# Macaron block, Mamba phase: the gated result stays in its PSUM banks, and the output projection moves to the middle of the slot

## What is computed

```python
proj = hidden_states @ W_in.T                      # z, x, B, C, dt
xBC = silu(conv1d(xBC, conv_w, kernel 4) + conv_b)
dt = softplus(dt + dt_bias); A = -exp(A_log)
Y_diag = einsum('bclhn,bcshn,bhcls,bcshp->bclhp', C_c, B_c, Lmat, x_dt)
Y_off  = einsum('bclhn,bhcpn,bhcl->bclhp', C_c, prev_states, exp(A_cum))
y = Y_diag + Y_off + D_param * x                   # x: the skip
g = y * silu(z)                                    # the gate
gn = g * rsqrt(mean(g * g) + eps) * norm_w
return gn @ W_out.T
```

## Time and profile before

| | |
|---|---|
| median of 3 runs | 2416.67 us (2415.77 to 2417.97) |
| the profiled execution: its own time | 2403.61 us |
| its span, first to last instruction | 2401.9 us |
| mean granted TensorE clock | 0.966 |
| the Mamba phase in it | about 380 to 2040 us |
| one group (two slots) in the loop | 47.8 us |

### The profile page before, as it was taken

How to read it: one execution, slowest core, us unless ns; L and a number is a source line. 1 busy time by engine, 2 the same in 40 slices (tenths; PEclk the granted TensorE clock), 3 DMA queues, 4 the chain that set the end, 5 groups by cost and what they waited for, 6 DMA issues and landing times. The chain is left out here.

```text
span 2401.9 us, 43273 instructions
## 1 busy us (share of the span) xinstructions
PE 2168.2 (90%) x11718; PEld 1748.5 (73%) x11718; DVE 1732.9 (72%) x2954; ACT 1430.8 (60%) x2899; POOL 1503.9 (63%) x1242
## 2 busy tenths in 40 slices
PE   5799987899999999999888999999999998579997
PEld 3687765677777777777666777777777776367776
DVE  6432276688888888888877888888888886743226
ACT  5133324777767776777566777677767774513332
POOL 2885341667767776777426777677767774288633
PEclk8999997999999999999999999999999999789999
DMA  9665351443334333333213334333433330266546
GB/s 340 238 188 168 116 157 41 115 113 92 92 103 107 92 97 102 102 92 100 60 39 111 94 90 104 105 95 89 105 105 95 88 105 18 75 241 189 160 135 193
DMA packets 204904, 285.32 MB, mean 119 GB/s; under 512 B 16288, under 2 KB 148458, under 8 KB 204816
## 3 DMA queue, kind: packets, MB, share of 16 engines
q1 hardware_dynamic: 185936, 219.18, 31.8%
q0 software_dynamic: 18880, 65.02, 8.7%
HBM read 225.43 MB, written 58.72 MB: 118 GB/s over the span
## 5 line engine op out<-in xcount | busy, mean ns | idle before, releaser
L2026 PE MATMUL mamba_p_proj<-mamba_xt_lo,mamba_in_hi 128*128 128x512 f32 x1056 | 462.6, 438 | 70.1 <-DVE mamba_xs L1706 52.2
L2028 PE MATMUL mamba_p_proj<-mamba_xt_hi,mamba_in_lo 128*128 128x512 f32 x1056 | 418.4, 396 | 0.0
L2027 PE MATMUL mamba_p_proj<-mamba_xt_hi,mamba_in_hi 128*128 128x512 f32 x1056 | 417.5, 395 | 0.0
L1315 POOL TENSOR_TENSOR mamba_mix<-mamba_mix,mamba_scores 128x512 f32<-128x512 f32 x256 | 372.3, 1455 | 70.0 <-ACT mamba_mix L1507 70.0
L1503 ACT ACTIVATE mamba_mix<-mamba_cum_l,mamba_cum_g 128x128 f32<-128x128 f32 x1024 | 324.5, 390 | 3.9 <-PE mamba_p_diag L2134 2.9
L1701 DVE SCALAR_TENSOR_TENSOR mamba_xs<-mamba_p_proj,mamba_taps,mamba_xs 128x511 f32<-128x511 f32 (+2 forms) x384 | 285.5, 744 | 46.2 <-ACT mamba_xs L1437 26.7
L2026 PEld LDWEIGHTS mamba_p_proj<-mamba_xt_lo,mamba_in_hi 128*128 128x128 f32 x1056 | 202.1, 191 | 129.4 <-DVE mamba_xs L1706 65.0
L1309 POOL TENSOR_TENSOR mamba_xend<-mamba_xdt,mamba_to_end_g 128x512 f32<-128x512 f32 x128 | 135.0, 1055 | 252.2 <-DVE mamba_xdt L1761 252.2
L1732 DVE TENSOR_TENSOR mamba_total<-mamba_p_out,mamba_total 128x512 f32<-128x512 f32 x256 | 176.4, 689 | 151.1 <-PE mamba_p_out L2062 150.9
L1322 POOL TENSOR_TENSOR mamba_decayed<-mamba_state,mamba_exp_last_g 128x256 f32<-128x256 f32 x192 | 181.8, 947 | 157.9 <-DVE mamba_state L1793 155.6
L660 DVE TENSOR_TENSOR ffn_h<-ffn_p_gu,ffn_sil 128x256 f32<-128x256 f32 x110 | 46.8, 426 | 294.3 <-ACT ffn_sil L545 293.9
(11 more groups left out here) (336 smaller groups left out, 5318.1 us busy)
## 6 DMA issues: line engine op xcount, KB each, us to landing
mamba_cum_l<-mamba_cum_rows SPq DMA_DIRECT2D x128, 512.0 KB, 5.6
mamba_rise<-mamba_exp_rows SPq DMA_DIRECT2D x256, 128.0 KB, 3.3
ffn_xs<-slots_in SPq DMA_DIRECT2D x78, 256.0 KB, 2.7
slots_out<-ffn_y SPq DMA_DIRECT2D x78, 256.0 KB, 2.5
mamba_raw_x<-in_t SPq DMA_DIRECT2D x34, 512.0 KB, 7.0
mamba_raw_z<-in_t SPq DMA_DIRECT2D x32, 512.0 KB, 7.8
mamba_raw_out<-out_t SPq DMA_DIRECT2D x32, 512.0 KB, 6.5
slots_out<-ffn_xs SPq DMA_DIRECT2D x1, 9984.0 KB, 42.3
```

The costliest lines, as they stand in the source:

```text
L1315: pool.tensor_tensor(mix[:, c, :, :], mix[:, c, :, :], scores[:, b * CPB + c, :].unsqueeze(1).broadcast_to([P, GH, P]), ALU.mult).then_inc ...
L2026: pe.matmul(bank, in_hi[:, piece, kk, :], xt_lo[:, kk, c], start=(kk == 0), stop=False)
L2027: pe.matmul(bank, in_hi[:, piece, kk, :], xt_hi[:, kk, c], start=False, stop=False)
L2028: last = pe.matmul(bank, in_lo[:, piece, kk, :], xt_hi[:, kk, c], start=False, stop=(kk == KT - 1))
```

## The change

A unit's result stays in the two banks that `diag` wrote, now named p_y: `add_skip`, `add_carry` and `gate` read and write p_y in place, ACT's square and g_hi and DVE's g_lo read it. All of this is done in the unit's own slot. So `diag` of the next unit waits for `gate_low` (s_glo) and no more for `add_skip` (s_y). ACT squares before it rounds. `project_out(U-1)` moves from the end of the slot to after `start(2)`, both `project_z` to after `off(3)`; the queues of the other engines are put in a matching order. A one-element Exp at the end of ACT's slot loads the table of exponentials there.

```diff
 # ACT
             def tap_x(k, gi, b, ct, young=False):
-                    act.wait_ge(s_g, U * CT - 2 * CT + ct + 1)
+                    act.wait_ge(s_y, U * CT - 2 * CT + ct + 1)
...
-            def high(U, gi, b, ct, second=False):
+            def square_and_high(U, gi, b, ct, first=False):
+
+                if ct == 0 and not first:
+                    act.wait_ge(s_pout, U * TPB)
                 act.wait_ge(s_g, U * CT + ct + 1)
-                if not second:
-                    act.wait_ge(s_pout, U * TPB)
-                act.activation(g_hi[:, ct, :], zs[:, b, ct, :], ACT.Copy,
+                act.activation(zs[:, b, ct, :], p_y[:, ct, :], ACT.Square).then_inc(s_sq, 1)
+                act.activation(g_hi[:, ct, :], p_y[:, ct, :], ACT.Copy,
                                scale=norm_w[:, bass.ds(gi * CT + ct, 1)]).then_inc(s_ghi, 1)
 # DVE
-                    dve.tensor_tensor(zs[:, b, ct, :], xs[:, b, ct, :], zs[:, b, ct, :], ALU.mult).then_inc(s_g, 1)
+                    dve.tensor_tensor(p_y[:, ct, :], p_y[:, ct, :], zs[:, b, ct, :], ALU.mult).then_inc(s_g, 1)
...
-                    dve.scalar_tensor_tensor(g_lo[:, ct, :], zs[:, b, ct, :], norm_w[:, bass.ds(gi * CT + ct, 1)],
+                    dve.scalar_tensor_tensor(g_lo[:, ct, :], p_y[:, ct, :], norm_w[:, bass.ds(gi * CT + ct, 1)],
...
-                    dve.scalar_tensor_tensor(xs[:, b, ct, :], xs[:, b, ct, :], skip[:, bass.ds(gi * CT + ct, 1)],
-                                             p_diag[:, ct, :], ALU.mult, ALU.add).then_inc(s_y, 1)
+                    dve.scalar_tensor_tensor(p_y[:, ct, :], xs[:, b, ct, :], skip[:, bass.ds(gi * CT + ct, 1)],
+                                             p_y[:, ct, :], ALU.mult, ALU.add).then_inc(s_y, 1)
...
-                    dve.tensor_tensor(xs[:, b, ct, lo:BLK], xs[:, b, ct, lo:BLK], carry[:, ct, lo:BLK],
+                    dve.tensor_tensor(p_y[:, ct, lo:BLK], p_y[:, ct, lo:BLK], carry[:, ct, lo:BLK],
 # PE
                     if j == 0 and not first:
-                        pe.wait_ge(s_y, U * CT)
+                        pe.wait_ge(s_glo, U * CT)
...
-                else:
-                    project_z(k, gn, bn, 0)
                 if first:
                     diag(1)
+                elif not last:
+                    project_out(k, gp, bp, range(TPB), second)
                 off(3)
                 start(3)
...
+                    project_z(k, gn, bn, 0)
+                    rows(k, gn, bn, 0)
                     project_z(k, gn, bn, 1)
-                    rows(k, gn, bn, 0)
-                    if not first:
-                        project_out(k, gp, bp, range(TPB), second)
-                if not last:
                     rows(k, gn, bn, 1)
```

More of the change, by code:

```diff
@@ L1363, in slot @@
                     decay_scores(U, b, 3)
-                clear(0)
-                next_z(0)
-                next_z(1)
                 this_out(0)
                 this_out(1)
+                clear(0)
+                if not first:
+                    for ct in range(CT):
+                        add_squares(U - 1, 1 - b, ct, second and ct == 0)
                 clear(1)
@@ L1585, in slot @@
                     silu_z(U + 1, 1 - b, 0, first)
-                    if b == 0 and not last_group:
-                        round_x(k, gi, V, 1)
+                for ct in range(CT):
+                    square_and_high(U, gi, b, ct, k == 0 and first)
+                if more:
+                    dt_copy(k + 1, 1)
+                if b == 0 and not last_group:
+                    round_z(k, gi, U, 0)
+                if not last:
                     silu_z(U + 1, 1 - b, 1, first)
-                    exponents(k, gn, bn, 3)
                 if b == 0 and not last_group:
-                    for ct in range(CT):
-                        round_z(k, gi, U, ct)
+                    round_z(k, gi, U, 1)
+                if not last:
+                    act.activation(spare, one[:, :], ACT.Exp)
             def vectors():
@@ L1835, in slot @@
                 next_state(0)
-                if not first:
-                    gate(k, gp, bp)
-                elif k > 0:
-                    finish(k - 1, range(6, T))
                 if b == 1 and not last:
                     stage_cum(k, gn)
+                if first and k > 0:
+                    finish(k - 1, range(6, T))
                 next_rows(0, 1)
@@ L1846, in slot @@
                 next_state(1)
-                if not first:
-                    gate_low(U - 1, gp, 1 - b)
                 next_rows(2, 3)
@@ L1861, in slot @@
                     add_out(1)
-                add_skip(1)
+                if not last:
+                    for t in range(CPB):
+                        add_out(t)
+                next_stats(1)
                 carry_of(3)
@@ L1866, in slot @@
                     add_carry(ct)
-                if not last:
+                gate(k, gi, b)
+                next_rows(6, 7)
+                if last:
+                    for t in range(2, CPB):
+                        add_out(t)
+                        if more:
+                            lns.low(dve, k + 1, T - CPB + t)
+                else:
                     if b == 1:
@@ L1870, in slot @@
                     times_dt(k, gn, bn, 0)
-                if more:
-                    gate(k, gi, b)
-                next_rows(6, 7)
-                for t in range(2 if last else 0, CPB):
-                    add_out(t)
-                    if more:
-                        lns.low(dve, k + 1, T - CPB + t)
-                if more:
-                    gate_low(U, gi, b)
+                gate_low(U, gi)
                 if not last:
```

73 lines of the change are left out of this document (27 added, 46 removed).

## The result

The changed kernel takes 2475.49 us (median of 4 runs, 2468.46 to 2478.83), the kernel before, on the same chip, 2416.57 us (4 runs, 2415.77 to 2417.97): a ratio of 1.024, 95% interval 1.0227 to 1.0253, so 2.4% slower. The profiled execution takes 2474.68 us with a span of 2472.8 and a granted clock of 0.952. Against the profiled execution of before (2403.61) it is 71 us longer, where the medians are 59 apart. The traces tell where the 71 lie. The Mamba phase, from PE's first to its last instruction in it, takes 1683.6 us before and 1737.6 after, 54.0 more. The other 17 us are in the feed-forward layers, whose code is the same (718.2 and 735.3 us in all).

The account below looks back on a forecast made before the run. PE, 90% busy, was taken to set the time. New accumulation waits of +131.7 us, less 68.8 and 4, give +59 us: 2416.7 + 59 = 2476 us, 2.4% slower; own range 2445 to 2504, wider range 2425 to 2504.

Parts of the forecast that it names:

- the named wait: Tile 2 of project_out on PE waits for DVE's accumulation of tile 0: 4.39 us new per slot pair, +131.7 us.
- the wait with b = 0: PE's new accumulation wait in b = 0 slots, halo steps held by POOL: 3.07 us; 1.49 with clean steps.
- What goes: PE's two waits for DVE's convolution before project_z vanish, -68.8 us; half the gate_low waits in batches' last slots, -4 us.
- The wait with b = 1: PE's new wait in b = 1 slots for DVE's accumulation before tile 2 of project_out: 1.32 us.
- its rounding comes after the next x projection; I cost this at nothing: SP's raw_x load still issued at the previous slot's carry, landing in 7.0 us, rounded later: no cost.
- the term of -4: Last slot of a batch: gate_low's late waits for project_out sum to 7.8 us; half taken as gone, -4 us.
- The 13 us carried over: The earlier runs' median stood 13 us above the profiled execution; kept, making 2463 into 2416.7 + 59 = 2476 us.
- The range: The forecast's own 2445 to 2504 us, for 0.7 us less or 0.9 us more waiting per slot pair.
- Gets cheaper but doesn't count.: gate on DVE falls from 1131 ns to 0.7 us with one input in PSUM; worth nothing by itself.
- The end of the slot: diag(0) waits for gate_low's read of p_y: 6.9 us chain hidden behind 9.0 us of PE projections, about 2 spare.
- rival 3: gate_low late for diag(0) on top of the forecast: at 1 us a slot +60, 2536 us; chance 0.06.
- Rival 2: Accumulation isn't waited for, faster: 2344 us; sign turns at a mean new wait of 1.21 us per slot; chance 0.12.

Follow-up runs that it names:

- runs 9 to 11: Changed kernel with DVE's accumulator additions earlier still and each batch's first round_x(0) behind tap_x(1), the middle one with SBUF tiles: 2330.10, 2330.39 and 2330.35 us.
- Run 4: Changed kernel with the small halo steps of ct 1 reading their PSUM bank in place of the SBUF halo tile: 2419.81 us, ratio 1.0015.
- Run 1: Changed kernel with DVE's accumulation of tiles 0 and 1 between the convolution steps of ct 1, except in a batch's last slot: 2366.93 us, ratio 0.9794.
- run 3: Changed kernel with two accumulator additions between the convolution steps of ct 1 in slots with b = 0 alone: 2403.84 us, ratio 0.9954.
- run 2: Changed kernel with two accumulator additions between the convolution steps of ct 1 in slots with b = 1 alone: 2412.96 us, ratio 0.9985.
- run 8: Changed kernel with round_x(0) moved back behind tap_x(1) on ACT in each batch's first slot: 2452.89 us, ratio 1.0208.
- run 7: Changed kernel's order, but skip, carry, gate and rest through SBUF tiles and squares at the end of ACT's slot: 2458.08 us, ratio 1.0228.
- run 10: Changed kernel with accumulator additions earlier, first-slot round_x(0) behind tap_x(1), results in SBUF tiles and squares at the end of ACT's slot: 2330.39 us, ratio 0.9694.
- Run 5: Changed kernel with project_out and its additions back at the end of the slot, results still in PSUM: 2659.03 us, ratio 1.1074.

## Why the prediction came out right, and where it was off

The time (2475.5 against 2476), the sign and the named wait are right. The total is nearer than the terms deserve: the wait with b = 0 was put some 30 us too high over the loop, and the fall of the clock, which was not in the sum, cost some 30. That they cancel is luck.

- **What goes.** Right. Both waits of the earlier trace rows are gone in the loop, and PE's own work of "about 45.6 us" a group is confirmed by the 45.80 of runs 9 to 11. By it the old waits were worth 47.79 - 45.80 = 1.99 us a group, where 2.15 was forecast.
- **The wait with b = 1.** Predicted 1.32 us, measured 1.26. The chain halo copy, tap, three steps with carry and state between them, accumulation was right step by step.
- **The wait with b = 0.** This term of the sum was mis-sized: 3.07 predicted, 2.11 measured. The timeline of DVE in the changed kernel at that place:

```profile
697.18 0.75 DVE L1688 SCALAR_TENSOR_TENSOR mamba_xs<-mamba_p_proj,mamba_taps,mamba_xs 128x511 f32<-128x511 f32 x1 [1.08 <-ACT mamba_xs L1437]
697.85 0.21 DVE L1693 SCALAR_TENSOR_TENSOR mamba_xs<-mamba_halo,mamba_taps,mamba_xs 128x1 f32<-128x1 f32 x1
...
699.29 0.53 DVE L1693 SCALAR_TENSOR_TENSOR mamba_xs<-mamba_halo,mamba_taps,mamba_xs 128x2 f32<-128x2 f32 x1
...
700.40 0.65 DVE L1693 SCALAR_TENSOR_TENSOR mamba_xs<-mamba_halo,mamba_taps,mamba_xs 128x3 f32<-128x3 f32 x1
700.97 1.27 DVE L1719 TENSOR_TENSOR mamba_total<-mamba_p_out,mamba_total 128x512 f32<-128x512 f32 x2
```

And POOL's at the same time:

```profile
699.20 0.60 POOL L1323 TENSOR_TENSOR mamba_decayed<-mamba_state,mamba_exp_last_g 128x256 f32<-128x256 f32 x1
699.76 1.26 POOL L1264 TENSOR_TENSOR mamba_in_lo<-mamba_raw_x,mamba_in_hi 128x512 fp32r<-128x512 f32 x1
```

`off(2)` starts at T = 695.92. The first step starts at T + 1.26 (predicted 1.11), the three pairs take 3.12 us (697.18 to 697.97 and 698.64 to 700.97; predicted 4.14, clean 2.56), and the accumulation starts at T + 5.05 instead of T + 5.91. I had taken the 4.14 us of the earlier trace rows over whole. They came from one meeting of two queues; in the new order the first halo step is free and the others are held for 0.3 and 0.4 us, to 699.82 and 701.05, just behind the ends of POOL's two instructions at 699.80 and 701.02. Run 4 puts the hold at 0.67 us a group, not 1.58. The estimate beside the forecast, made by the rule of the Trainium skill (SBUF — State Buffer, "Who interferes with whom") with arrivals at random, was 2.75 us; the trace agrees with the rule that the halo steps are still held, and both the number taken from rows and the estimate are above the 2.11 measured.
- **Not in the sum: the clock.** A fall to 0.62 behind the second of two waits, in 19 of 30 groups, 1.56 us each, some 30 us in all. Runs 1, 3 and 4 show that it goes when the wait with b = 0 gets shorter, run 2 that it nearly goes (3 of 30) without the other.
- **Not in the sum: the batch's first slot.** I costed the load and rounding of raw_x at nothing from the loop alone. In the first slot the transfer isn't there yet, and run 8 gets 5 to 8 us back. Here the step "its rounding comes after the next x projection; I cost this at nothing" failed.
- **The balance.** In the loop the forecast was 131.7 - 68.8 = +63; the regular groups grew by 65 over 30, of which the waits are 3.37 - 1.99 = 1.38 us a group and the clock about 1.0 (together 0.2 more than the 2.17 measured). The edges of the batches take 10 off, to +55. In the last slots of the batches the two waits for `gate_low` in the slot (0.77 and 3.17 us) are gone, as the term of -4 had it, and the phase behind unit 31 is 3.5 us shorter at the end. A new wait of 3.2 us for `gate_low` stands between the batches, where the next batch's dt projection writes p_y. Between the batches it is +2.8, ahead of unit 1 -0.3. That makes +54 in the Mamba phase, beside +59 forecast and +59 between the medians of the same chip.
- **The 13 us carried over.** The forecast added them because the profiled execution of before lay that much under its median. By the traces (see the result) they lie in the feed-forward layers and go with the chip; no trace of the kernel before was taken on the chip of the medians, so this is argued. The carry was right, though for no reason that the prediction had.
- **The range.** Its lower end doesn't follow from the text beside it: 0.7 us less per pair is 21 us, 2455 and not 2445.
- **"Gets cheaper but doesn't count."** The value (0.69 us measured for `gate`) and the verdict are right, and runs 7 and 10 show the verdict directly (`gate` takes 699 and 698 ns there with both inputs in SBUF). The reason that I gave, one input in PSUM, is wrong for `gate`: see below.
- **The end of the slot, rival 3.** Right that `diag(0)` wouldn't wait for `gate_low`; no such wait comes in the loop. Run 5 shows why the cover mattered: without it the kernel is 10.7% slower, by a path over ACT's queue that I hadn't priced.
- **Rival 2** asked for a mean wait under 1.21 us a slot. The measured one is 92.0 / 60 = 1.53 (1.69 by the delay of tile 2). Run 4, with 70.6 us in 60 waits, 1.18 each, lands on no change (1.0015), which is where that threshold puts it. Run 1, with 0.3 us a slot, is faster.

## What to carry to other kernels

When a producer is moved up in one engine's queue, look at once at how its consumers' additions stand in the other engine's queue: a double-buffered output needs the first one drained before the third tile, and two short additions moved ahead of a convolution were worth more (4.4%) than the whole change cost. When a stage does more in its own slot, follow every "may I overwrite" wait to the queue that holds it, since everything behind it pays. And price the first iteration apart from the loop: a transfer that is hidden in the steady state may be the longest wait of the first.

## What the runs showed of the hardware that was not expected

- The granted TensorE clock (1.00 is 2.4 GHz) fell to the lower level, 1.2 GHz, for a part of the 4.44 us behind a wait of 2 us, 0.62 on the mean, in a stretch in which PE was otherwise busy; with the same wait and no 1.26 us wait the slot before (run 2) it stayed at 1.00 in all but three of 30 groups, and with waits of 1.3 us at most (run 4) in all. Two waits of 1.3 and 2.1 us thus cost 1.0 us a group more than their length (19 falls of 1.56 us in 30 groups).
- `gate` with both inputs in SBUF took 1131 ns before, and the same instruction 698 ns in run 10, where POOL stands still at that place. DVE in run 10, by shape, and POOL around one pair of gates (699.29 to 700.57):

```profile
L1717 DVE SCALAR_TENSOR_TENSOR mamba_g_lo<-mamba_zs,mamba_norm_w,mamba_g_hi 128x512 fp32r<-128x512 f32 x128 | 139.2, 1113 | 1.5 <-ACT mamba_g_hi L1469 0.4
...
L1712 DVE TENSOR_TENSOR mamba_zs<-mamba_xs,mamba_zs 128x512 f32<-128x512 f32 x128 | 84.3, 698 | 0.0
```

```profile
695.65 2.55 POOL L1316 TENSOR_TENSOR mamba_mix<-mamba_mix,mamba_scores 128x512 f32<-128x512 f32 x2
701.77 1.53 POOL L1310 TENSOR_TENSOR mamba_xend<-mamba_xdt,mamba_to_end_g 128x512 f32<-128x512 f32 x1 [3.56 <-DVE mamba_xdt L1753]
```

Its place made it cheaper, not the bank. `gate_low` is the opposite case: 1113 ns with SBUF inputs beside a working POOL, and 751 ns when one input is in PSUM (96.1 us for 128 in the changed kernel). So for these two instructions a PSUM input keeps DVE clear of POOL, and is worth nothing where POOL is idle.
